# Attention with two passes of scores: how far row scores run ahead of key scores in the second and third quads of heads

## The reference

```python
q, k, v = heads(x @ Wq.T + bq), heads(x @ Wk.T + bk), heads(x @ Wv.T + bv)   # 16 heads of 16, T = 4096, D = 256
q, k = rope(q), rope(k)
att = softmax(where(tril, q @ k.T / 4, -inf))
x = layernorm(x + (att @ v) @ Wo.T + bo)
h = silu((x @ w1.T) * s1) * ((x @ w2.T) * s2)        # 1024 wide
h = gelu((h @ h1.T) * hs1); h = gelu((h @ h2.T) * hs2)
out = layernorm(x + (h @ w3.T) * s3)
```

## Time and profile before

| what | us |
|---|---|
| median of 3 runs (lowest 3042.97, highest 3045.86) | 3043.56 |
| the profiled execution: its time | 3041.05 |
| the profiled execution: its span | 3039.3 |
| TensorE busy | 2854.9 |
| VectorE busy | 2061.7 |
| ScalarE busy | 1302.8 |
| copy of the output of (0,0), and of (3,0), the last | 241.22, 1867.81 |

### The profile page before, as it was taken

The page is one execution under the profiler, slowest core; times in us unless marked ns, Lnnn a source line. Parts: engine busy times, 40 slices in busy tenths (PEclk is TensorE's granted clock), DMA queues, the critical chain, the costliest instruction groups (busy, mean ns, idle before and its releaser), DMA issues. The chain is left out here.

```text
span 3039.3 us, 40625 instructions
## 1 busy us (share of the span) xinstructions
PE 2854.9 (94%) x15648; PEld 1509.0 (50%) x15648; DVE 2061.7 (68%) x3638; ACT 1302.8 (43%) x2545; POOL 95.5 (3%) x122
## 2 busy tenths in 40 slices
PE   8949999999999989999999996499999998999998
PEld 4423333333333323333333331377777777888887
DVE  7979999887777779998877761554445554435333
ACT  0005666777777656667777774011111111100010
POOL 0030200020000200000000000000000000000000
PEclk9959999999999989999999998699999999999999
DMA  5441440025000250000000002311111013211200
GB/s 163 152 94 37 61 60 5 5 36 71 5 5 9 40 79 8 5 5 5 5 5 5 5 9 73 97 56 56 55 55 55 35 41 134 92 42 48 76 14 21
DMA packets 86620, 138.35 MB, mean 46 GB/s; under 512 B 27744, under 2 KB 57312, under 8 KB 83776
## 3 DMA queue, kind: packets, MB, share of 16 engines
q1 hardware_dynamic: 73504, 96.25, 9.7%
q0 software_dynamic: 5472, 23.34, 6.1%
q10 hardware_dynamic: 7488, 16.65, 1.7%
HBM read 85.22 MB, written 50.99 MB: 45 GB/s over the span
## 5 line engine op out<-in xcount | busy, mean ns | idle before, releaser
L506 DVE TENSOR_REDUCE at_segmax<-at_row 128x1 f32<-128x512 f32 (+3 forms) x2304 | 1329.6, 638 | 256.6 <-PE at_row L436 188.4
L559 ACT ACTIVATE at_probs<-at_key 128x512 f32<-128x512 f32 (+3 forms) x2304 | 1136.8, 566 | 543.6 <-PE at_key L452 373.9
L436 PE MATMUL at_row<-at_k_stack,at_q_stack 96*128 96x512 bf16 (+3 forms) x2304 | 810.4, 370 | 34.2 <-POOL at_values L362 28.4
L452 PE MATMUL at_key<-at_q_stack,at_k_stack 99*128 99x512 bf16 (+3 forms) x2304 | 811.7, 364 | 20.5 <-DMA at_q_stack<-maxima 11.8
L471 PE MATMUL at_o<-at_probs,at_values 128*32 128x512 f32 (+2 forms) x4608 | 575.0, 571 | 0.0
L436 PEld LDWEIGHTS at_row<-at_k_stack,at_q_stack 96*128 96x128 bf16 x2304 | 222.8, 98 | 594.8 <-DVE at_segmax L506 409.6
L452 PEld LDWEIGHTS at_key<-at_q_stack,at_k_stack 99*128 99x128 bf16 x2304 | 224.3, 98 | 278.9 <-ACT at_probs L559 130.6
L782 PE MATMUL wi_f<-wi_h_h,wi_h1w_h 128*128 128x512 f32 x512 | 206.8, 404 | 10.5 <-DVE wi_h_l L913 10.5
L1091 ACT ACTIVATE na_h3f<-na_h,na_hs 128x512 f32<-128x512 f32 x64 | 44.1, 689 | 401.9 <-PE na_h L1056 401.9
L1056 PE MATMUL na_h<-na_h_h,fr_h2w_h 128*128 128x512 f32 x512 | 203.4, 397 | 5.7 <-DVE na_h_l L1106 5.4
L1056 PE MATMUL na_h<-na_h_l,fr_h2w_h 128*128 128x512 f32 x512 | 202.7, 396 | 0.0
(11 more groups left out here) (108 smaller groups left out, 2414.5 us busy)
## 6 DMA issues: line engine op xcount, KB each, us to landing
hidden<-wi_h SPq DMA_DIRECT2D x64, 256.0 KB, 2.0
at_q_stack<-q_parts POOLq DMA_DIRECT2D x72, 128.0 KB, 23.8
at_k_stack<-k_parts POOLq DMA_DIRECT2D x18, 512.0 KB, 28.5
outputs<-at_outs SPq DMA_DIRECT2D x32, 256.0 KB, 2.0
fr_o<-outputs SPq DMA_DIRECT2D x8, 1024.0 KB, 5.9
fr_h2f<-hidden SPq DMA_DIRECT2D x4, 2048.0 KB, 9.2
na_h2f<-hidden SPq DMA_DIRECT2D x4, 2048.0 KB, 9.5
q_parts<-pr_parts SPq DMA_DIRECT2D x48, 128.0 KB, 1.9
```

Source lines behind the costliest of these rows:

```text
L436: last = nc.tensor.matmul(bank[:, 0:w], qst[u][0:SROWS, c, h, i * P:(i + 1) * P], kst[u][0:SROWS, h, s * CH:s * CH + w], start=True, stop= ...
L452: last = nc.tensor.matmul(bank[:, q0:CH], kst[u][0:SROWS + PARTS, h, j * P:(j + 1) * P], qst[u][0:SROWS + PARTS, c, h, q0:CH], start=True, ...
L506: nc.vector.tensor_reduce(segmax[:, n % 2, h * TPC + i, s:s + 1], row_ps[r % RING_R][:, 0:w], op=ALU.max, axis=AX.X).then_inc(rows_taken, 1)
L559: nc.scalar.activation(probs[:, g % RING_P, h, q0:CH], key_ps[m % RING_K][:, q0:CH], ACT.Exp).then_inc(probs_ready, 1)
```

## The change

```diff
--- before.py
+++ after.py
@@ -272,7 +272,10 @@
             if (j, h) == (0, 0):
                 start = key_cols
             rise = size[n + 1] if n + 1 < NQUAD * NCH else 0
-            goal = min(total, start + size[n] + SLACK + (key_cols - start) * rise // size[n])
+            lead = size[n] + (key_cols - start) * (rise - size[n]) // size[n]
+            if blocks[n][0] not in (0, NQUAD - 1):
+                lead = max(size)
+            goal = min(total, key_cols + lead + SLACK)
             while r < len(rows) and (row_cols < goal or rows[r][1] == TURN):
                 m, i, _, s = rows[r]
                 row_cols += 0 if i == TURN else row_width(blocks[m][1], i, s)
```

## The result

The changed kernel takes 3020.07 us (median of 4 runs, 3018.17 to 3025.77), the kernel before, measured beside it, 3043.33. The ratio is 0.9925 with a 95% interval of 0.9908 to 0.9942, so 17.6 to 28 us are gone. 3022.3 was predicted, in a range from 3016 to 3031. The profiled execution took 3021.08 us, 20.0 less than that of before.

What follows compares the result with a forecast made beforehand. TensorE, busy 94% of the span, was taken as the bound, so gains come only from its waits or lower clock. 13.6 + 7.7 + 0 = 21.3 us off gave a forecast of 3022.3 us, range 3016 to 3031.

Steps and rivals of the forecast that it cites:

- Term 1: Block (2,1): TensorE's wait for the maxima copies of (2,2), and the half clock behind it, go: -13.6 us.
- The twin that gave 13.6: Block (0,1), same keys and row columns as (2,1): 28.39 against 42.03 us, so 13.64 belong to (2,1)'s place.
- No maxima are in flight while q0 loads: End of quad 1: the pair of (2,3) goes out early, then four outputs, so no maxima copies meet quad 3's load.
- needed 76,800 columns later: Maxima in flight in the new order: needed some 106 us later, against 12.75 + 15.1 us for the copies.
- Term 2: Blocks (2,0) to (2,6): with r = 1, excess over TensorE's bill falls from 15.2 to 7.5 us: -7.7 us.
- the 0.86 from 1120 to 1130 us: Start of quad 2: granted clock falls though TensorE is busy all the time, shortly after the stall.
- the floor of 1.0 us a block: From (0,7) and (1,7): a block where TensorE is fed takes 1.0 us more than its bill.
- Term 3: Quad 1: 3 us gained in small blocks against 3 lost in (1,4): 0, with bounds of -5 and +6.
- Part of it hides: Block (1,4): VectorE billed 51.8 us, TensorE 57.6, so four closings' 2.3 to 5.6 us partly hide; 3 us taken.
- only the stall goes: Rival, quad 2: excess is bunching, not VectorE's rate, and turns up in (1,4) and (1,3); 3030 us, chance 0.12.
- The changed transfer: Rival, start of quad 2: output stores slowed beside quad 3's load make TensorE wait; 3036 us, chance 0.06.
- the lasting loss of 34 us: Clock rival, (1,4) and (1,3): short waits bring 1.2 GHz for a third of their bill; 3056 us, chance 0.02.

Runs made afterwards that it cites:

- e9_load_in_gap: Kernel before, with GpSimd's load of quad 3 put off until it starts with block (2,6): 3035.01 us, ratio 0.9963.
- e1_load_late: Kernel before, with GpSimd's load of quad 3 waiting for the end of block (2,2) instead of (1,0): 3047.79 us, ratio 1.0009.
- e6_floor_middle: Changed kernel, with the lead in quads 1 and 2 following block size but not below chunk 3's block: 3029.75 us, ratio 0.9960.
- e3_half_scans: e1_load_late, with VectorE scanning half the columns of the row scores of (2,1) to (2,7) and (3,7): 3032.43 us, ratio 0.9962.

## Why the prediction was right

**Term 1, the stall and its clock: 13.6 us predicted.** Right in size: e9_load_in_gap takes 42.03 to 28.40, with 0.6 us of it back in (2,2); e1_load_late, with the lower clock in (2,1), shows 29.80. The twin that gave 13.6 was one of three profiled (0,1) at full clock; the seven others would have given 12.2 to 12.6. The reason given was right in its cause, the copies beside the load, and wrong in three things. The load lasts some 60 us, not 48. "No maxima are in flight while q0 loads" is not so, the pair of (2,4) is. And "needed 76,800 columns later" is too much: the margin is the lead less the size of the block, 76,800 - 37,888 columns or by the estimate 54 us for (2,4). The trace has 57.5 (1119.97 to about 1177.5), of which 43.7 were left when the spill ended. e6_floor_middle shows that the difference matters: the same mistake made me expect its lead of 61 us to be enough.

**Term 2, VectorE's part of quad 2: 7.7 us predicted.** The excess over TensorE's bill from (2,0) to (2,6), without the stall, fell from 15.2 us to 5.7 (307.0 us taken, 301.3 billed): 9.5 us. e3_half_scans shows that it is VectorE's rate. About 1.4 of them came by way of the clock: the 0.86 from 1120 to 1130 us, which the prediction read as an after-effect of the stall, follows TensorE's wait before the transpose at 1116.88, and the twin (0,2) has the same stretch (0.96 over the block) with no stall anywhere near. The size was a little under, as the floor of 1.0 us a block was read from (0,7) and (1,7), each of which has a closing in it; (2,0) and (2,1), which have none, came to less than 0.5 each.

**Term 3, quad 1: 0 predicted, between -5 and +6.** The excess went from 13.4 to 14.0 us (410.3 taken, 396.3 billed). Inside, both sides were larger than said: the three small blocks (1,2) to (1,0) gained 4.8 us, not 2 to 3, and (1,5) and (1,4) lost 5.7, 4.6 of them in (1,4), not 3. "Part of it hides" was the step that failed there: nearly nothing of the closings hid, since by the prediction's own bill a group with a closing gives VectorE 4.0 to 4.2 us of work for 3.2 to 3.4 of TensorE's. The three groups with a transpose took 4.64, 5.17 and 5.09 us and hold nearly all of (1,4)'s excess. That the two sides cancelled to 0.6 us was luck.

The sum over the blocks is 13.6 + 9.5 - 0.6 = 22.5 us, 21.3 predicted. **The rivals:** only the stall goes (3030) is out by the blocks of quad 2 and by e3_half_scans. The changed transfer was nearer than its chance says, by its own mark: two stores took 17.3 and 19.0 us in the load, and 20 were named as the point from which it would decide. But ScalarE needs the buffer of (2,0)'s store, free at about 1098, only for the output of (2,2) at 1134. The clock stayed at 1.00 from (0,2) to (3,3) of the changed kernel, also in (1,4), where row scores go round their four banks with waits of up to 1.14 us. It was not at 1.00 everywhere: with a wait of 1.38 us before a transpose, (0,1) of the same profile had 0.94. The Trainium skill says in "TensorE: Matmul & The Clock Gate", section "A second HAM failure mode: psum-queue depth-cycling", that a TensorE which idles briefly between groups as it goes round its banks swings between the two levels. The traces bear that out in part: there are such stretches, but they cost 1.0 to 1.5 us each, and the lasting loss of 34 us that the rival took from the rule does not show.

## What to carry to other kernels

Where one pass of work prepares something for another through DRAM, the margin of a piece is the lead less the piece's own size; compare that, not the lead, with how long the round trip takes while the largest load runs. A lead that follows the size of the pieces also makes the rate of the feeding engine follow it: count its work for a group at the steepest place, not on the average. And a chain of tiny operations on a busy engine costs its length wherever the queue in front of it is short, so put it on an engine that is idle.

## What the hardware did that I had not expected

How long a copy took beside the load hardly depended on its size. 12 KB spills took 12.75, 13.2, 13.8 and 15.1 us in four runs beside a load that filled some 90% or more of the DMA engines, and 1.3 to 1.4 alone; 256 KB stores took 17.3, 19.0 and 19.5 there, and 2.0 alone. And GpSimd did the short operations on 16 columns (0.20 to 0.22 us each, one every 0.28) nearly as fast as VectorE (0.17, one every 0.21).

A wait of 1.4 us was enough to bring TensorE's lower clock, and not each time. Block (2,1) waited 1.38 us before the same transpose in e1_load_late and in e9_load_in_gap; the granted clock of the block was 0.94 in the one and 1.00 in the other, and the block took 29.80 and 28.40 us. In (3,2) the wait of 1.93 us went with 31.7 us in some profiles and 30.6 in others in the same way. In (0,2) and (2,2) of the kernel before, a wait of 0.58 us before the transpose was followed by the lower clock (0.96 over the block), and in (1,4) of the changed kernel 1.14 and twice 0.96 were not. What decides is not shown.
